# RWKV mixing and scan in one section of the program, with key-value products kept in PSUM

## The reference

```python
x5 = xn[:, :, None] + sx[:, :, None] * (maa_stack + xxx)          # five mixed inputs
w = jnp.exp(-jnp.exp(time_decay + jnp.tanh(x5[:, :, 1] @ decay_w1) @ decay_w2))
r, k, v = x5[:, :, 3] @ Wr.T, x5[:, :, 0] @ Wk.T, x5[:, :, 2] @ Wv.T
g = jax.nn.silu(x5[:, :, 4] @ Wg.T)
def step(s, rkvw):
    r_t, k_t, v_t, w_t = rkvw
    a = k_t[:, :, :, None] * v_t[:, :, None, :]
    out = jnp.einsum('bhk,bhkd->bhd', r_t, u * a + s)              # u is faaaa, the bonus
    return (a + w_t[:, :, :, None] * s, out)
att = ((a4 - m) * jax.lax.rsqrt(var + EPS)).reshape(b, l, E) * gn_w + gn_b   # norm per head
x = x + att * g @ Wo.T
```

## Time and profile before

| what | value |
|---|---|
| median of the runs | 1342.48 us |
| profiled execution | 1343.32 us, span 1341.6 us |
| TensorE, VectorE busy | 1184.0 us (88%), 871.7 us (65%) |
| ScalarE, GpSimd busy | 636.0 us (47%), 647.6 us (48%) |
| mixing, first to last instruction | 761.4 to 831.9 us |
| scan section up to its layer norm | 832.2 to 956 us |

### The profile page before, as it was taken

The page is one execution under the profiler, slowest core; times in us unless marked ns, Lnnn a source line. Parts: engine busy times, 40 slices in busy tenths (PEclk is TensorE's granted clock), DMA queues, the critical chain, the costliest instruction groups (busy, mean ns, idle before and its releaser), DMA issues. The chain is left out here.

```text
span 1341.6 us, 20628 instructions
## 1 busy us (share of the span) xinstructions
PE 1184.0 (88%) x7388; PEld 907.9 (68%) x7388; DVE 871.7 (65%) x2094; ACT 636.0 (47%) x1425; POOL 647.6 (48%) x673
## 2 busy tenths in 40 slices
PE   6999999999999999999989688766658998899994
PEld 4887888888888788888877533422445775666664
DVE  5776666766667666676665343997555565766666
ACT  3655565555655555655542123002123673477770
POOL 3565665656556565565751031442001672277760
PEclk9999999999999999999999789797799899999997
DMA  5110211101111011210102000000030000000000
GB/s 199 64 48 17 64 64 63 49 17 63 64 64 48 19 61 64 63 48 25 55 17 78 16 1 0 1 0 0 0 88 0 1 2 1 1 1 2 1 2 32
DMA packets 35111, 47.06 MB, mean 35 GB/s; under 512 B 3865, under 2 KB 22082, under 8 KB 35010
## 3 DMA queue, kind: packets, MB, share of 16 engines
q1 hardware_dynamic: 34640, 44.83, 10.4%
q10 hardware_dynamic: 370, 0.91, 0.2%
HBM read 44.69 MB, written 1.05 MB: 34 GB/s over the span
## 5 line engine op out<-in xcount | busy, mean ns | idle before, releaser
L444 POOL TENSOR_TENSOR a_prob<-a_prob,a_inv_total 128x512 f32<-128x512 f32 x128 | 144.1, 1126 | 217.6 <-DVE a_inv_total L732 217.6
L1593 POOL TENSOR_TENSOR l_scores<-l_scores,l_neg_max 128x512 f32<-128x512 f32 x144 | 147.8, 1040 | 99.1 <-DVE l_neg_max L1583 98.8
L1583 DVE CUSTOM_DVE_ANT_0 l_scores<-psum,mask 128x256 f32<-128x256 f32 x384 | 139.8, 421 | 69.6 <-PE psum L1536 69.6
L637 ACT ACTIVATE a_prob<-psum,a_neg_max 128x257 f32<-128x257 f32 x256 | 118.9, 472 | 93.0 <-DVE a_neg_max L729 92.0
L1614 ACT ACTIVATE l_prob_T<-psum 128x512 f32<-128x512 f32 x192 | 108.8, 590 | 34.3 <-PE psum L1550 34.3
L1550 PE MATMUL psum<-ident,l_scores 128*128 128x128 f32 x768 | 116.4, 290 | 7.0 <-POOL l_scores L1593 3.9
L1550 PEld LDWEIGHTS psum<-ident,l_scores 128*128 128x128 f32 x768 | 85.1, 145 | 41.1 <-issue 18.8
L736 DVE TENSOR_TENSOR a_probT_lo<-psum,a_probT_hi 128x512 fp32r<-128x512 f32 x128 | 87.9, 687 | 23.0 <-ACT a_probT_hi L641 22.5
L729 DVE TENSOR_REDUCE a_neg_max<-psum 128x2 f32<-128x514 f32 x128 | 87.3, 682 | 1.3 <-PE psum L486 1.3
L566 PE MATMUL psum<-ident,a_prob 128*128 128x128 f32 x512 | 77.6, 274 | 6.8 <-POOL a_prob_bias L447 6.8
L641 ACT ACTIVATE a_probT_hi<-psum 128x512 fp32r<-128x512 f32 x128 | 76.6, 599 | 9.3 <-PE psum L566 9.3
(11 more groups left out here) (322 smaller groups left out, 3325.4 us busy)
## 6 DMA issues: line engine op xcount, KB each, us to landing
wk_raw<-in_L_xattn_wk SPq DMA_DIRECT2D x16, 512.0 KB, 6.4
wq_raw<-in_L_xattn_wq SPq DMA_DIRECT2D x16, 512.0 KB, 5.7
wv_raw<-in_L_xattn_wv SPq DMA_DIRECT2D x16, 512.0 KB, 3.7
wo_raw<-in_L_xattn_wo SPq DMA_DIRECT2D x16, 512.0 KB, 4.1
ctx_rows<-in_ctx SPq DMA_DIRECT2D x3, 512.0 KB, 4.2
x_rows<-in_x SPq DMA_DIRECT2D x2, 512.0 KB, 9.5
mask<-in_mask_Bx1xSxS_ff SPq DMA_DIRECT2D x1, 1024.0 KB, 8.0
out_dram<-fin_y SPq DMA_DIRECT2D x4, 256.0 KB, 2.1
```

The costliest lines, as they stand in the source:

```text
L444: pool.tensor_tensor(prob[:, m % 4, :, 0:S], prob[:, m % 4, :, 0:S], rtot[:, m % 4, :].unsqueeze(2).to_broadcast([P, 2, S]), ALU.mult)
L637: act.activation(prob[:, m % 4, q, 0:S + 1], s_bank(g)[:, q, 0:S + 1], ACT.Exp, bias=negm[:, m % 4, q:q + 1], accum_out=tot[:, m % 4, q:q ...
L1583: e = dve.tensor_tensor_reduce(sc[:, i % SC, q, :], s_bank(i)[:, q * S:(q + 1) * S], masks[:, b * NM + q % NM, :], 1.0, BIG, ALU.add, ALU. ...
L1593: pool.tensor_tensor(sc[:, i % SC, :, :], sc[:, i % SC, :, :], m[:, i % SC, :].unsqueeze(2).to_broadcast([P, 2, S]), ALU.subtract).then_in ...
```

## The change

The two stages become one function, stage_rwkv, with one section per engine and no barrier inside.

- VectorE builds spread and gather right after mix_first, GpSimd same_head before its first mixed product.
- ScalarE rounds v per chunk right behind pv; VectorE takes v_lo of each chunk in front of the g products of that chunk.
- TensorE makes the spread of e=0 in front of pr, the spread of e=1 in front of pg 0 and pg 2. Products from pv on use banks 4 to 7, the spread banks 0 to 3.
- VectorE's scan goes chunk by chunk: two kv, the starting state, one scan. The kv products are written over the spread in PSUM, and the scan reads them there. The gate products of g stand behind e=1.
- The bonus term: ScalarE multiplies k with faaaa (into mix_first), GpSimd multiplies with r behind z of e=0, and with v behind z of e=3 and e=4. VectorE has none of it.
- GpSimd's z waits for its own chunk's scan, no longer for both. z, ruk, ru, att and sq lie in tensors of the mixing that are no longer read; the layer norm's rows too.

```diff
-def stage_rwkv_mix(chip, m, xe, kT, vT, rT, wT, gT):
+def stage_rwkv(chip, m, xe, kT, vT, rT, wT, gT, make_ln):
...
+        ruk, ru = first, mixed[:, 0]
+        z = [mixed[:, 2], sx[:, :, :, :].rearrange("p c b s -> p c (b s)")]
+        att, sq = scaled[:, 0], scaled[:, 1]
+        dec = flat(first[0:KD, 0, :, :])
+        tanh_of = lambda n: (th if n < 2 else e1)[:, n % 2, :]
...
+        BANKS = {'low': (0, 1, 2, 3), 'mw': (4, 5, 6, 7), 'mk': (0, 1, 2, 3), 'd1': (4, 5), 'mv': (6, 7, 0, 1), 'mr': (2, 3, 4, 5),
+                 'pk': (6, 7, 0, 1), 'd2': (2, 3, 4, 5), 'pv': (6, 7, 4, 5), 'mg': (6, 7, 4, 5), 'pr': (6, 7, 4, 5), 'pg': (6, 7, 4, 5)}
...
+                def spread_values(e, c):
+
+                    if c == 0:
+                        pe.wait_ge(spread_ok, e + 1)
+                    if e == 0:
+                        pe.wait_ge(v_lo_ok, c + 1)
+                        pe.wait_ge(act_free, nth(num['d2', 1]))
+                    else:
+                        pe.wait_ge(st_ok, (e - 1) * NC + c + 1)
+                    for n in (2 * c, 2 * c + 1):
+                        out = batches(ps[:, n, :])
+                        pe.matmul(out, spread[:, e, :], v_hi[:, c, bh(n), 0:S], start=True, stop=False)
+                        pe.matmul(out, spread[:, e, :], v_lo[:, c, bh(n), 0:S], start=False, stop=True).then_inc(v_full, 1)
...
+                    if key == ('pr', 0):
+                        spread_values(0, 0)
+                        spread_values(0, 1)
+                    if key == ('pg', 0):
+                        spread_values(1, 0)
+                    if key == ('pg', 2):
+                        spread_values(1, 1)
...
+                for e in range(2, S1 + LATE):
+                    if e < S1:
+                        for c in range(NC):
+                            spread_values(e, c)
+                    if e == 2:
+                        pe.wait_ge(ruk_ok, NC)
+                        pe.wait_ge(dve_free, nth(num['pg', 3]))
+                        for n in range(4):
+                            pe.matmul(ps[:, 4 + n, :], same[:, :], flat(ruk[:, n // 2, bh(n), :]), start=True, stop=True).then_inc(ru_full, 1)
+                    g = e - LATE
+                    if g == 0:
+                        pe.wait_ge(gather_ok, S1)
+
+                        pe.wait_ge(ru_read, 4)
+                    pe.wait_ge(z_ok, NC * g + NC)
+                    for n in SEQ:
+                        mm = pe.matmul(ps[:, 4 + n, :], gather[:, g, :], z[g % 2][:, n // 2, half(n)], start=g == 0, stop=g == S1 - 1)
+                        if g == S1 - 1:
+                            mm.then_inc(g_full, 1)
+                    if g < S1 - 1:
+                        mm.then_inc(g_full, 1)
...
+                def values_low(c):
+                    dve.wait_ge(v_hi_ok, c + 1)
+                    dve.tensor_tensor(v_lo[:, c, :, 0:R1], vT[:, c, :, :], v_hi[:, c, :, 0:R1].bitcast(F32), ALU.subtract).then_inc(v_lo_ok, 1)
...
+                        if x == 'g' and n % 2 == 0:
+                            values_low(n // 2)
+                        scale(i, x, n)
...
+                for e in range(S1):
+                    for c in range(NC):
+                        for n in (2 * c, 2 * c + 1):
+                            dve.wait_ge(v_full, 4 * e + n + 1)
+                            dve.tensor_tensor(batches(ps[:, n, :]), kT[:, c, bh(n), 0:S], batches(ps[:, n, :]), ALU.mult).then_inc(kv_ok, 1)
+                        dve.wait_ge(kv_ok, 4 * e + 2 * c + 2)
+                        dve.tensor_copy(batches(kv_of(c))[:, :, 0:1], m['s0'][:, c, :, e:e + 1]).then_inc(s0_ok, 1)
+                        dve.wait_ge(s0_ok, e * NC + c + 1)
+                        if e >= 2:
+                            dve.wait_ge(z_ok, (e - 2) * NC + c + 1)
+                        dve.tensor_tensor_scan(flat(state[:, e % 2, c, :, :]), flat(wT[:, c, :, :]), kv_of(c), 0.0, ALU.mult, ALU.add).then_inc(st_ok, 1)
+                    if e == 1:
+                        for n in range(4):
+
+                            c, h = ch(n)
+                            dve.wait_ge(th_ok, n + 1)
+                            dve.scalar_tensor_tensor(gT[:, c, half(n)], tanh_of(n), 1.0, ps[:, bank_of(('pg', n)), :], ALU.add, ALU.mult).then_inc(dve_free, 1)
...
+                pool.wait_ge(act_free, nth(num['pr', 3]))
+                for e in range(S1):
+                    if e >= 2:
+                        pool.wait_ge(g_full, e - 1)
+                    for c in range(NC):
+                        pool.wait_ge(st_ok, e * NC + c + 1)
+                        pool.tensor_tensor(z[e % 2][:, c, :], rT[:, c, :], flat(state[:, e % 2, c, :, :]), ALU.mult).then_inc(z_ok, 1)
+                    if e == 0:
+                        for c in range(NC):
+                            pool.wait_ge(uk_ok, c + 1)
+                            pool.tensor_tensor(flat(ruk[:, c, :, :]), rT[:, c, :], flat(ruk[:, c, :, :]), ALU.mult).then_inc(ruk_ok, 1)
+                    if e in (3, 4):
+                        c = e - 3
+                        pool.wait_ge(ru_read, 4)
+                        pool.tensor_tensor(batches(att[:, c, :]), batches(ru[:, c, :]), vT[:, c, :, 1:R1], ALU.mult).then_inc(ru_v, 1)
+                ln.gpsimd(pool)
...
+                        if what == 'pv' and h == 1:
+                            act.wait_ge(act_free, nth(i))
+                            act.wait_ge(mats_zero, 3)
+                            act.activation(v_hi[:, c, :, 0:R1], vT[:, c, :, :], ACT.Copy).then_inc(v_hi_ok, 1)
...
+                        if h == 1:
+                            act.activation(ruk[:, c, :, :], kT[:, c, :, 1:R1], ACT.Identity, scale=chip.vec('L1_xattn_faaaa', c)).then_inc(uk_ok, 1)
...
-                    stage_rwkv_mix(chip, m, xe, kT, vT, rT, wT, gT)
-                    stage_rwkv_scan(chip, m, kT, vT, rT, wT, gT, ln_l1(2))
+                    stage_rwkv(chip, m, xe, kT, vT, rT, wT, gT, ln_l1(2))
```

More of the change, by code:

```diff
@@ L879, in stage_rwkv_mix @@
         mixed = sb("mixed", [P, 3, NC, TOK])
-        dec = sb("dec", [KD, TOK])
         e1 = sb("e1", [P, 2, BANK])
         th = sb("th", [P, 2, BANK])
+        same = sb("same_head", [P, P])
+        dmask = sb("d_mask", [P, S1])
+        spread = sb("spread", [P, S1, P], F32R)
+        gather = sb("gather", [P, S1, P])
+        v_hi, v_lo = sb("v_hi", [P, NC, B, R1 + 1], F32R), sb("v_lo", [P, NC, B, R1 + 1], F32R)
+        state = sb("state", [P, 2, NC, B, S])
+        epsc = sb("eps", [P, 1])
         cur = lambda c: xe[:, c, :, 1:R1]
@@ L955, in _ @@
                         product(key, w['W' + what[1]], slice((n // 2) * P, (n // 2 + 1) * P), lambda c: mixed[:, i % 3, c, half(n)])
+                for e in range(2, S1 + LATE):
[18 more added lines that the diff above has]
+                        mm.then_inc(g_full, 1)
+                for i, n in enumerate(SEQ):
+                    pe.wait_ge(att_ok, i + 1)
+                    pe.matmul(ps[:, n, :], same[:, :], att[:, n // 2, half(n)], start=True, stop=True).then_inc(mean_full, 1)
+                for i, n in enumerate(SEQ):
+                    pe.wait_ge(sq_ok, i + 1)
+                    pe.matmul(ps[:, 4 + n, :], same[:, :], sq[:, n // 2, half(n)], start=True, stop=True).then_inc(var_full, 1)
+                for t in range(NT):
+                    if t % 4 == 0:
+                        pe.wait_ge(gated, 2 + 2 * (t // 4))
+                        pe.wait_ge(log_ok, 4)
+                    for c in range(NC):
+                        mm = pe.matmul(ps[:, 4 + t // 2, (t % 2) * D:(t % 2 + 1) * D], z[0][:, c, t * P:(t + 1) * P], w['Wo'][:, c, :], start=c == 0, stop=c == NC - 1)
+                    if t % 2:
+                        mm.then_inc(o_full, 1)
+                ln.tensor(pe)
             @block.vector
@@ new lines, in centre @@
+                def centre(i):
+                    n = SEQ[i]
+                    dve.wait_ge(mean_full, i + 1)
+                    dve.scalar_tensor_tensor(att[:, n // 2, half(n)], ps[:, n, :], -1.0 / S1, att[:, n // 2, half(n)], ALU.mult, ALU.add).then_inc(cent_ok, 1)
+                dve.wait_ge(ru_v, NC)
+                for i, n in enumerate(SEQ):
+                    dve.wait_ge(g_full, S1 + i)
+                    dve.tensor_tensor(att[:, n // 2, half(n)], att[:, n // 2, half(n)], ps[:, 4 + n, :], ALU.add).then_inc(att_ok, 1)
+                    if i >= 2:
+                        centre(i - 2)
@@ L985, in _ @@
+                gate(3)
+                for q in range(4):
+                    dve.wait_ge(o_full, q + 1)
+                    dve.scalar_tensor_tensor(chip.x[:, 2 * q:2 * q + 2, :], ps[:, 4 + q, :].rearrange("p (j n) -> p j n", j=2), 0.5,
+                                             chip.x[:, 2 * q:2 * q + 2, :], ALU.mult, ALU.add).then_inc(x_ok, 1)
+                    ln.after_rows(dve, q)
             @block.gpsimd
@@ L998, in _ @@
                     c, h = ch(n)
[L999 removed]
```

(5 more changed lines are left out.)

240 lines of the change are left out of this document (53 added, 187 removed).

## The result

| | time, us | ratio to before, 95% |
|---|---|---|
| predicted | 1308.0 (1303 to 1321) | |
| before, this comparison (4 runs) | 1342.12 (1340.95 to 1343.86) | |
| after (4 runs) | 1308.63 (1308.19 to 1309.12) | 0.9741 (0.9728 to 0.9755) |

The profiled execution of after took 1308.19, with a span of 1306.5.

What follows compares the result with a forecast made beforehand. Two bounds in series, TensorE in the mixing and VectorE in the scan, with a barrier between. -20.8 (start) - 9.6 (scan) - 3.2 (end) - 1.5 (gather clock) + 0.6 (selects) = -34.5, giving 1308.0 us, range 1303 to 1321.

Steps and rivals of the forecast that it cites:

- the start: From the mixing to the first kv: first kv at 817.8 us, 20.8 earlier, with +0.6 for the selects.
- the scan: First kv to last scan: 64.4 us instead of 74.0, 9.6 less, at 3.73 per chunk.
- the end: Behind the last scan: one z left before gather 7, 3.2 us less, and 1.5 less from gather 7's clock.
- The term for the selects: Start of the mixing: two selects building same_head collide with VectorE's first work, +0.6 us, bounds 0 and 0.8.
- Waits for TensorE: VectorE waits at e=1 (0.3 and 0.4), at the gate products (0.4) and at e=3 (0.9), together 2.0 us.
- The loop through gather 0: At e=2, z and ruk, then ru and gather 0 delay the spread of e=3; VectorE waits 0.9 us.
- No standing behind GpSimd: In the scan, VectorE's about 12 us of standing behind GpSimd goes; taken as 0 left, other end +15.
- idle under 20% from e=1 on: GpSimd in the scan: idle under 20% from e=1, with 47 us of work from 824.6 to 884, 80% full.
- (a): TensorE's clock at the low level in two or three scan periods: +7 to +11 us, about 1317; 12%.
- (b): Scan or copy still fights GpSimd for the port: +15 to +19 us, 1323 to 1327; 10%.
- (c): VectorE pays double for PSUM in kv and scan: together +52 us, 1360; 3%.
- (d): The order doesn't overlap: GpSimd's wait for r blocks z, hence the scan of e=2; about 1320 us; 5%.

Runs made afterwards that it cites:

- experiment 6: Changed kernel with only TensorE's order altered: values of steps 1, 3 and 4 spread earlier or in halves around the first gathers; 1304.83 us, ratio 0.9707.
- (4): Kernel before with only kv, the starting state and the scan moved to PSUM, chunk by chunk; 1332.64 us, ratio 0.9925.
- experiment 1: Changed kernel with kv and the starting state written to SBUF and scanned from there; 1335.53 us, ratio 0.9946.
- Experiment 5: Changed kernel with the starting state added in PSUM by small TensorE matmuls instead of VectorE's 16 copies; 1311.51 us, ratio 0.9755.
- 7: Changed kernel with kv in SBUF and scanned from there, the starting state added in PSUM by TensorE, no VectorE copy; 1327.86 us, ratio 0.9886.
- 2: Changed kernel with the four gate products ahead of the scan and the spread of e=1 behind pg; 1322.37 us, ratio 0.9843.
- 3: Changed kernel with the bonus term back on VectorE; 1315.20 us, ratio 0.9794.
- 9: Changed kernel with GpSimd zeroing the gather matrix behind its selects and VectorE doing the last z; 1307.01 us, ratio 0.9722.

## Why the prediction was right

The mechanism held in all three parts. That 1308.0 was met to 0.6 is partly luck: the terms were off by up to 0.6 each way and cancelled, and before alone ranges over 3 us. The section shows the agreement better, -34.4 for -34.5, as -20.7, -9.3 and -4.4 for the start, the scan and the end, where -20.2, -9.6 and -4.7 were forecast.

**Start.** Right to 0.5. The first kv was to be 20.2 earlier on balance and is 20.7. The term for the selects was too small and incomplete: the selects stretched the two SBUF operations beside them by 0.2 together, and the copy before them took 1.08 instead of 0.18 beside the memset of the gather matrix, which the prediction didn't price at all. That is 1.1, not 0.6. Of this, 0.8 was given back by TensorE's clock, which is luck: the first low-rank product took 8.90 after at a mean clock of 0.81 and 9.46 before at 0.76, the first decay product 5.07 and 5.35.

**Waits for TensorE.** Foreseen at the right four places: 0.3, 0.4, 0.4, 0.9; measured 0.76, 0.54, 0, 1.28. The sum is 2.6 instead of 2.0. TensorE was to begin pr at 816.8 and began at 817.56, behind spread products at the lower clock. The loop through gather 0 was right: spread of step 3 starts at 843.40, behind it. Experiment 6 shows that these waits were on the path.

**No standing behind GpSimd.** Right, and shown both ways: PSUM alone frees the old kernel (4), SBUF alone binds the new one (1). The rule cited from the Trainium skill (SBUF — State Buffer, "Who interferes with whom") holds for scan and copy: 2287 and 173 ns at most here, 4420 and 2067 in experiment 1. Pitch 3.71 for 3.73. The scan from PSUM takes 2285 to 2287 ns. Unheld from SBUF it took 2259 at least and 2280 in the median before, and 2291 to 2292 in experiment 1, where the source alone differs. kv written to PSUM takes 684, 10 more than the 674 of experiment 1. By the rule of the Trainium skill (VectorE: DVE Perf Modes, "The TRN2 errata"), the scan would have been 65 ns longer; no pair of rows shows that, and the measurement decides.

**GpSimd.** The work was sized right: 79% busy from 825.41 to 884.06, where 80% was forecast. The sign given for it, idle under 20% from e=1 on, did not come: its idle times add up to 12.1 of the 49.3 us from 834.72 to 884.06, 25%, the longest of them 4.65 at 844.04, in the loop through gather 0. The lags behind the bonus products did not reach VectorE, which has no wait from 844.46 to the last scan.

**End.** Right. The last gather starts 2.46 behind the last scan (2.4 predicted) and takes 3.70 instead of 5.16.

**Rivals.** (a) The lower clock came, but only in 814 to 818, ahead of pr and not in the periods of the scan; it is 1.00 from 818 to 890. The eight spread products of step 0 took 3.4 us there and those of step 3, at full clock, 2.25. So by an estimate from these rows it cost VectorE at most 1.2, inside the two first waits. Experiment 5 shows that this risk was real: with the small matmuls in step 0, in 5 and 7, pr took 8.26 and 8.12, in after and 1, 2, 3 and 9, without them, 7.05 to 7.28. (b) was priced too low: standing still costs 27, by experiment 1, not 15 to 19, since the price left out a scan held behind a held copy, and GpSimd's own standing. The kernel before showed the second, in a row that the prediction did not use: beside r * k * faaaa on VectorE, whose sources lie in SBUF, a pair of z took 6.59 for 4.71.

```profile
846.05 6.59 POOL L1089 TENSOR_TENSOR scan_z<-r_T,scan_state 128x1024 f32<-128x1024 f32 x2 [11.81 <-DVE scan_state L1118]
```

(c) is out by the durations (kv 697 ns at most, scan 2287), (d) by z of step 0 starting at 825.41.

## What to carry to other kernels

When VectorE and GpSimd take turns in a trace, look at how many operands of VectorE's instruction lie in SBUF, and move one to PSUM; price the conflict per pair of instructions on both engines, the small copies too, and not as one remainder per step. Where a stage bound by one engine is followed by one bound by another, put the second's first steps into the first's, and then write out the order of the engine that feeds both: its spreads in front of work that nobody waits for yet were worth another 2 us here (experiment 6). And compare milestones inside the changed stretch before reading a gain of a microsecond from the whole time. A small operation is not free on an idle engine if that engine is full at the time when the chain starts.
